# Filling the half-height last chunk of 704 gated values with zeros, up to 128 rows

## The chip, the cores and the metric

The kernel runs on one core of a Trainium2 chip. The metric is the device time of one execution in microseconds (us). The engines are TensorE (PE; its weight loads are listed apart as PEld), VectorE (DVE), ScalarE (ACT), GpSimd (POOL) and SyncE (SP), and SyncE issues most of the DMAs.

## The reference, cut to what matters

Four layers run one after the other on x of shape (4, 512, 256), each a cross-attention and a feed-forward. Two of the feed-forwards have a hidden width of 704. The first layer's is a mixture of 8 experts, two per token:

```python
B, T, D, F = (4, 512, 256, 704)
gate = jnp.einsum('bted,edf->btef', dispatched, gate_proj)
up = jnp.einsum('bted,edf->btef', dispatched, up_proj)
acts = jax.nn.silu(gate) * up
expert_out = jnp.einsum('btef,efd->bted', acts, down_proj)
```

The third layer's rounds its input, its weights and its hidden values to fp4, in blocks of 16 values with one scale each:

```python
gate = fp4_linear(x, w_gate)
y = fp4_linear(x, w_up)
h = jax.nn.silu(gate) * y
return fp4_linear(h, w_down)
```

704 is five and a half times 128. The product with the down weights sums over these 704 values.

## The kernel before

Both places cut the 704 hidden values into FC = 6 chunks: FULL = 5 of 128 rows and a last one of LEFT = 64 rows (FW holds the heights). A chunk stands with its rows on the partitions, and TensorE sums over them.

**The blocks of the first layer** (function `blocks`, names that begin with e0b_). Tokens are sorted by expert into NB = 39 blocks of 128 rows. For each block n TensorE does `gate(n)` (into gp), `turn_rows(n + 1)` (transposes the next block's rows, into xp), `up_product(n)` (into up) and `down(n - 1)` (into yp). An fp32 matmul of the program is two records in the trace, each with its weight load: gate is 24 records with 128 columns, turn_rows 2, up 20, and down 12 with 256 columns, of which the last two are the half-height chunk. The gate product's sixth chunk holds 64 gate columns and, beneath them, the first 64 up columns, so it is full. DVE multiplies (`hidden`: five chunks, then the half chunk) into hT[j], copies the transposed rows (`copy_rows`) and the result (`copy_out`), and every two blocks it does one round of fp4 rounding of the third layer's weights (f2w_). ACT applies silu. SP loads each block's weights into double buffers: wgu[j] is reloaded when `up_product(n)` has ended, for block n + 2, and wd[j] when `down(n)` has. The last layer (e3b_) uses the same function with F = 512, which has no half chunk; for it the new wait and memsets are not made.

**The fp4 feed-forward** (function `lookup_and_feed_forward`, names f_ and f2w_). T = 16 tiles of 128 tokens. The order of TensorE is written out by hand; for tile n it is `gate_up(n)` (tails of 192 columns, then gp, up, then the tails of up, which wait for ACT's silu of the first tails), `turn_rows(n + 1)`, `down(n - 2)`, `turn_hidden(n - 1)`, and in some tiles the parts of a nearest-neighbour lookup. DVE does the multiplication `hidden(n)`, then the rounding of the hidden values of tile n and of the rows of tile n + 2 (some 8 us), then the statistics of tile n - 3 and `add(n - 2)`, which reads yp. POOL ends both roundings (f_hq, f_xq). `turn_hidden` transposes hq by chunks into two groups, hp (four chunks) and hx (chunk 4 and the half chunk, which is a matmul with 64 stationary columns), and ACT's `copy_hidden` takes them to hT: one copy of four chunks, one of chunk 4, one of the half chunk. `down` is 12 records of 256 columns, as in the blocks.

Each stage ends with a barrier, and POOL then clears the stage's semaphores one by one.

Of the kernel before, what the change touches and what calls it, by code (L numbers as in the profile page):

```python
# [21 lines left out]
P = 128  # L22
# [103 lines left out]
def build(nc, ctx, ins, out):  # L126
# [2033 lines left out]
    def blocks(tag, w_gate, w_up, w_down, F, NB, experts_n, owner, token, rounds=None, pair=None):  # L2160
# [14 lines left out]
        with ExitStack() as st:  # L2175
# [22 lines left out]
            if pair is None:  # L2198
# [3 lines left out]
            x_turned, x_copied, gate_made, up_made, sg_done, h_done, y_made, y_copied = (  # L2202
                sem(n) for n in ("xt", "xc", "gate", "up", "sg", "h", "ymade", "yc"))
            DN = 16 if F % P == 0 else 32

            with nc.Block() as block:
                @block.sync
# [90 lines left out]
                @block.tensor  # L2298
                def _(pe):
                    def turn_rows(n, j, count):  # L2300
                        pe.wait_ge(rows_in[j], 16 * before[j] + 16 * count)
                        for k in range(KC):
                            last = nc.tensor.transpose(xp[:, k, :], xb[j][:, k * P:(k + 1) * P], ident)  # L2303
                        last.then_inc(x_turned, 1)

                    def product(at, chunks, dst, j, done):
                        for f in range(chunks):
                            for k in range(KC):
                                last = nc.tensor.matmul(dst[:, f, :], wgu[j][:, k, at + f * P:at + (f + 1) * P], xT[j][:, k, :],  # L2309
                                                        start=(k == 0), stop=(k == KC - 1))  # L2310
                        last.then_inc(done, 1)

                    def gate(n, j, count):
                        pe.wait_ge(x_copied, n + 1)
                        pe.wait_ge(gu_in[j], 32 * count)
                        if positive(n):
                            pe.wait_ge(h_done if LEFT else sg_done, n)
                        product(0, FC, gp, j, gate_made)

                    def up_product(n, j):  # L2320
                        if positive(n):
                            pe.wait_ge(h_done, n)
                        product(F + LEFT, FULL, up, j, up_made)

                    def down(n, j, count):
                        pe.wait_ge(d_in[j], DN * count)
                        pe.wait_ge(y_copied, n + 1)
                        pe.wait_ge(h_done, n + 1)
                        for f in range(FC):
                            last = nc.tensor.matmul(yp[:], hT[j][0:FW[f], f, :], wd[j][0:FW[f], f, :], start=(f == 0),  # L2330
                                                    stop=(f == FC - 1))
                        last.then_inc(y_made, 1)

                    def body(i, last_block=False):
                        for j in (1, 0):
                            n = i * 2 + 2 - j
                            gate(n, j, i + 2 - j)
                            if not (last_block and j == 0):
                                turn_rows(n + 1, 1 - j, i + 2)
                            up_product(n, j)  # L2340
                            down(n - 1, 1 - j, i + 1)

                    stay_busy(gp[:, 0:4, :].rearrange("p f c -> p (f c)"), 30)
                    turn_rows(0, 0, 1)
                    gate(0, 0, 1)
                    turn_rows(1, 1, 1)
                    up_product(0, 0)
                    with pe.Fori(0, NB // 2 - 1) as i:
                        body(i)
                    body(NB // 2 - 1, last_block=True)  # L2350
                    down(NB - 1, 0, NB // 2 + 1)
# [16 lines left out]
                @block.vector  # L2368
                def _(dve):
                    def copy_rows(n, j):  # L2370
                        dve.wait_ge(x_turned, n + 2)
                        nc.vector.tensor_copy(xT[j][:], xp[:]).then_inc(x_copied, 1)  # L2372

                    def hidden(n, j):
                        dve.wait_ge(sg_done, n + 1)
                        dve.wait_ge(up_made, n + 2)
                        for rows, chunks in PIECES:
                            from_up = up[rows, chunks, :] if chunks.start == 0 else gp[P - LEFT:P, chunks, :]
                            last = nc.vector.tensor_tensor(hT[j][rows, chunks, :], from_up, sg[rows, chunks, :], ALU.mult)  # L2379
                        last.then_inc(h_done, 1)  # L2380

                    def copy_out(n, j, count):
                        dve.wait_ge(y_made, n + 2)
                        if positive(count):
                            dve.wait_ge(stored[j], 16 * stored_before[j] + 16 * count)
                        nc.vector.tensor_copy(yb[j][:], yp[:]).then_inc(y_copied, 1)

                    copy_rows(0, 0)
                    copy_rows(1, 1)
                    hidden(0, 0)  # L2390
                    def body(i, last_block=False):
                        for j in (1, 0):
                            n = i * 2 + 2 - j
                            if not (last_block and j == 0):
                                copy_rows(n + 1, 1 - j)
                            hidden(n, j)
                            copy_out(n - 1, 1 - j, i)
                        if rounds is not None and not last_block:
                            rounds.round(dve, i)
                    body(0)  # L2400
                    with dve.Fori(1, NB // 2 - 1) as i:
                        body(i)
                    body(NB // 2 - 1, last_block=True)
                    copy_out(NB - 1, 0, NB // 2)
# [304 lines left out]
    def lookup_and_feed_forward(tag, layer, wt, slot, NB, F, weights):  # L2709
# [4 lines left out]
        with ExitStack() as st:  # L2714
# [10 lines left out]
            moments, root, rstd, shift = ([tmp(f"{n}{k}", s) for k in range(2)] for n, s in (  # L2725
                ("moments", [P, T, 2]), ("root", [P, T]), ("rstd", [P, T]), ("shift", [P, T])))
            xq, xT, sg, h, hq, hT = tmp("xq", [P, D]), tmp("xT", [P, KC, P]), tmp("sg", [P, F]), tmp("h", [P, F]), \
                tmp("hq", [P, F]), tmp("hT", [P, FC, P])
            x_bufs, h_bufs = quantise_buffers(tmp, D), quantise_buffers(tmp, F)
            cb = [ps(f"cb{j}", [P, S]) for j in range(2)]  # L2730
            gp, up, tails, hp0, hx, yp = ps("gp", [P, FM]), ps("up", [P, FM]), ps("tails", [P, 2, FT]), ps("hp", [P, 4, P]), \
# [10 lines left out]
                    "num", "hot", "ht", "hc", "p", "added", "recnt"))  # L2742
            aggregated, rooted, inverted, shifted, xn_ready = ([sem(f"{n}{k}") for k in range(2)] for n in (
                "agg", "root", "inv", "shift", "xn"))
            x_steps, h_steps, both_steps, x_quant, x_turned, x_copied, tail_made, gate_made, up_made, sg_tail, sg_done, h_done, h_quant, \
                h_turned, h_copied, y_made, y_added = (sem(n) for n in (
                    "xs", "hs", "bs", "xq", "xt", "xc", "tail", "gate", "up", "sgt", "sg", "h", "hq", "ft", "fc", "y", "ya"))
# [10 lines left out]
                return (xq[:], xn[:, n, :], D, x_bufs, x_quant, n)  # L2758

            def hidden_job(n):  # L2760
                return (hq[:], h[:], F, h_bufs, h_quant, n)

            with nc.Block() as block:
                @block.gpsimd
# [38 lines left out]
                def _(act):  # L2803
# [43 lines left out]
                    def copy_hidden(n):  # L2847
                        if n:
                            act.wait_ge(y_made, n)
                        for g, chunks in enumerate(groups):  # L2850
                            act.wait_ge(h_turned, n * NG + g + 1)
                            full = [f for f in chunks if FW[f] == P]
                            last = nc.scalar.copy(hT[:, full[0]:full[-1] + 1, :], hp[g][:, 0:len(full), :])
                            for f in chunks:
                                if FW[f] < P:
                                    last = nc.scalar.copy(hT[0:FW[f], f, :], hp[g][0:FW[f], f % 4, :])
                            last.then_inc(h_copied, 1)

                    act.preload_act_table(ACT.Sqrt)
                    act.wait_ge(summed, 1)  # L2860
# [38 lines left out]
                def _(dve):  # L2899
# [65 lines left out]
                    def statistics(n):  # L2965
                        dve.wait_ge(y_added, n + 1)
                        nc.vector.bn_stats(st6[:, n, :], x[:, n, :])

                    for b in range(B):
                        nc.vector.tensor_tensor(sqc[:, b, :], ctx_tok[:, b, :], ctx_tok[:, b, :], ALU.mult).then_inc(c_step, 1)  # L2970
                    dve.wait_ge(c_step, B)
# [52 lines left out]
                def _(pe):  # L3024
# [64 lines left out]
                    def turn_hidden(n):  # L3089
                        pe.wait_ge(h_quant, n + 1)  # L3090
                        for g, chunks in enumerate(groups):
# [2 lines left out]
                            if g:  # L3094
                                pe.wait_ge(x_copied, min(n + 3, T))
                            for f in chunks:
                                last = nc.tensor.transpose(hp[g][0:FW[f], f % 4, :], hq[:, f * P:f * P + FW[f]], ident)
                            last.then_inc(h_turned, 1)

                    def down(n):  # L3100
                        if n:
                            pe.wait_ge(y_added, n)
                        for g, chunks in enumerate(groups):
                            pe.wait_ge(h_copied, n * NG + g + 1)
                            for f in chunks:
                                last = nc.tensor.matmul(yp[:], hT[0:FW[f], f, :], dT[0:FW[f], f, :], start=(f == 0),
                                                        stop=(f == FC - 1))
                        last.then_inc(y_made, 1)

                    pe.wait_ge(c_step, B + 3)  # L3110
                    for b in range(B):
                        for k in range(KC):
# [93 lines left out]
```

## Time and profile before

| | before |
|---|---|
| runs, median (3) | 1820.89 us |
| runs, lowest to highest | 1820.48 to 1825.39 us |
| profiled execution, first to last instruction | 1819.4 us |
| PE busy | 1573.1 us (86%) |
| DVE busy | 983.0 us (54%) |
| ACT / POOL busy | 483.2 / 401.9 us |
| mean granted TensorE clock | 0.944 of 2.4 GHz |

The span of the profiled execution is 1.5 us under the median of the runs; the runs have no profile of their own. An engine's share is a mean over stages that differ, so it says little about any one of them. A record's length is not what it costs a stream of matmuls, because they are pipelined: what counts is the time from one start to the next.

### The profile page before, as it was taken

What the parts mean: (1) busy time and instruction counts of PE and PEld (TensorE: products, weight loads), DVE (VectorE), ACT (ScalarE), POOL (GpSimd) and SP (SyncE); (2) the same over time, 40 slices, a digit from 0 to 9 for tenths busy, and PEclk for the clock granted to TensorE, in tenths of its full rate; (3) what the DMA queues carried; (4) which work ended last, traced back from release to release, by engine and by line L of the source; (5) the groups of instructions that cost most, each with busy time, mean ns of one, the idle gap of its engine ahead of it and who ended that gap; (6) DMA issues with size and microseconds to landing.
All of it is one profiled execution on the core that took longest, in us unless ns stands there. A gap on an engine that the chain in (4) does not pass through costs nothing. (4 is left out here: it accounts for less than half of the span.)

```text
span 1819.4 us, 33679 instructions
## 1 busy us (share of the span) xinstructions
PE 1573.1 (86%) x11798; PEld 1136.1 (62%) x11830; DVE 983.0 (54%) x2513; ACT 483.2 (27%) x1045; POOL 401.9 (22%) x734
## 2 busy tenths in 40 slices
PE   5878999999968988799979899668888887999992
PEld 3654888889857743355544555445655664798992
DVE  4555344444369957766646333479887456222224
ACT  2331101101066631355522111223331431111010
POOL 0102211111042001111102244333111111344440
PEclk9999999999969999899999999878999999999996
DMA  4104888988721007234315132210000001799995
GB/s 141 38 2 145 302 300 292 308 293 301 231 62 36 2 1 195 82 85 110 82 32 168 33 81 77 70 38 18 1 1 1 1 2 47 260 315 318 314 320 187
DMA packets 162223, 240.64 MB, mean 132 GB/s; under 512 B 19808, under 2 KB 109344, under 8 KB 161984
## 3 DMA queue, kind: packets, MB, share of 16 engines
q1 hardware_dynamic: 149440, 208.35, 35.4%
q0 software_dynamic: 10512, 28.72, 5.8%
q10 hardware_dynamic: 2160, 2.10, 0.3%
q8 instruction: 69, 1.13, 0.3%
q14 instruction: 42, 0.34, 0.1%
HBM read 208.96 MB, written 30.15 MB: 131 GB/s over the span
## 5 line engine op out<-in xcount | busy, mean ns | idle before, releaser
L1543 DVE TENSOR_REDUCE l1a_nm<-l1a_sc 128x1 f32<-128x512 f32 (+3 forms) x256 | 107.1, 482 | 53.7 <-PE l1a_sc L1679 53.7
L2309 PEld LDWEIGHTS e0b_gp<-e0b_xT,e0b_wgu 128*128 128x128 f32 x936 | 107.4, 192 | 14.5 <-issue 12.3
L2309 PE MATMUL e0b_gp<-e0b_xT,e0b_wgu 128*128 128x128 f32 x936 | 114.9, 279 | 1.8 <-DVE e0b_hT L2379 1.3
L2330 PE MATMUL e0b_yp<-e0b_wd,e0b_hT 128*128 128x256 f32 x468 | 115.1, 388 | 0.6 <-issue 0.6
L2360 ACT ACTIVATE e0b_sg<-e0b_gp 128x640 f32<-128x640 f32 x78 | 33.5, 481 | 285.3 <-PE e0b_gp L2309 285.3
L2330 PEld LDWEIGHTS e0b_yp<-e0b_wd,e0b_hT 128*128 128x128 f32 x468 | 82.6, 189 | 21.9 <-issue 13.9
L2309 PE MATMUL e0b_up<-e0b_xT,e0b_wgu 128*128 128x128 f32 x780 | 93.5, 275 | 0.0
L2309 PEld LDWEIGHTS e0b_up<-e0b_xT,e0b_wgu 128*128 128x128 f32 x780 | 90.2, 192 | 0.0
L2309 PE MATMUL e3b_gp<-e3b_xT,e3b_wgu 128*128 128x128 f32 x624 | 78.1, 278 | 5.9 <-DMA e3b_wgu<-in_L_ffn_W 4.8
L2309 PEld LDWEIGHTS e3b_gp<-e3b_xT,e3b_wgu 128*128 128x128 f32 x624 | 73.9, 192 | 14.7 <-DMA e3b_wgu<-in_L_ffn_W 7.3
L2464 PE MATMUL e1b_gu<-e_kgu,e1b_xT 128*128 x152 | 75.2, 617 | 4.4 <-DVE e1b_xT L2529 2.8
L2360 ACT ACTIVATE e3b_sg<-e3b_gp 128x512 f32<-128x512 f32 x39 | 23.3, 597 | 206.3 <-PE e3b_gp L2309 206.3
L2309 PE MATMUL e3b_up<-e3b_xT,e3b_wgu 128*128 128x128 f32 x624 | 76.0, 275 | 0.0
L2330 PE MATMUL e3b_yp<-e3b_wd,e3b_hT 128*128 128x256 f32 x312 | 73.9, 380 | 0.6 <-issue 0.6
L2309 PEld LDWEIGHTS e3b_up<-e3b_xT,e3b_wgu 128*128 128x128 f32 x624 | 72.7, 192 | 0.0
L2379 DVE TENSOR_TENSOR e0b_hT<-e0b_up,e0b_sg 128x640 f32<-128x640 f32 x39 | 32.1, 824 | 64.2 <-PE e0b_up L2309 64.2
L1679 PE MATMUL l1a_sc<-causal_h,ident_h 128*128 128x128 bf16 x256 | 47.0, 223 | 20.0 <-PEq L1325 15.6
L1677 PEld LDWEIGHTS l1a_sc<-l_stack_k,l_stack_q 128*128 128x128 bf16 x256 | 25.3, 99 | 61.0 <-issue 27.2
L2330 PEld LDWEIGHTS e3b_yp<-e3b_wd,e3b_hT 128*128 128x128 f32 x312 | 56.3, 190 | 7.0 <-issue 0.9
L2372 DVE COPY e3b_xT<-e3b_xp 128x256 f32<-128x256 f32 x39 | 16.5, 424 | 78.8 <-PE e3b_xp L2303 78.8
L1206 DVE TENSOR_REDUCE a_nm<-a_sc 128x8 f32<-128x512 f32 x64 | 39.7, 682 | 35.8 <-PE a_sc L1056 35.8
L2259 POOL COPY e0b_index<-e_token 128x1 uint32 (+1 forms) x39 | 7.1, 182 | 233.6 <-PE e0b_xp L2303 228.8
(606 smaller groups left out, 3536.3 us busy)
## 6 DMA issues: line engine op xcount, KB each, us to landing
e3b_wgu<-in_L_ffn_W SPq DMA_DIRECT2D x78, 512.0 KB, 5.3
e0b_wgu<-in_L_ffn_gate_proj SPq DMA_DIRECT2D x39, 704.0 KB, 4.4
e0b_wgu<-in_L_ffn_up_proj SPq DMA_DIRECT2D x39, 704.0 KB, 5.8
e0b_wd<-in_L_ffn_down_proj SPq DMA_DIRECT2D x39, 640.0 KB, 5.2
e3b_wd<-in_L_ffn_W SPq DMA_DIRECT2D x39, 512.0 KB, 6.9
x_rows<-xn SPq DMA_DIRECT2D x3, 2048.0 KB, 8.6
l_parts<-l1p_split SPq DMA_DIRECT2D x16, 384.0 KB, 3.1
l_stack_k<-l_parts SPq DMA_DIRECT2D x48, 128.0 KB, 2.8
```

Of the source, the lines that this page charges most:

```text
L1206: nc.vector.tensor_reduce(nm[:, :, r, :], bank[r][:].rearrange("p t (h l) -> p t h l", l=L), AX_X, ALU.max, negate=True).then_inc(max_done, 1)
L1543: nc.vector.tensor_reduce(nm[:, g % 2, q, i:i + 1], sc[q], AX_X, ALU.max, negate=True).then_inc(max_done, 1)
L1677: nc.tensor.matmul(sc[q], of_head(1, n)[:, q * P:(q + 1) * P], of_head(0, n)[:, 0:(q + 1) * P], start=True, stop=False)
L1679: last = nc.tensor.matmul(sc[q][:, q * P:(q + 1) * P], ident_h[:], causal_h[:], start=False, stop=True)
L2259: nc.gpsimd.tensor_copy(index[j][:], token[:, bass.ds(n, 1)]).then_inc(index_ready, 1)
L2309: last = nc.tensor.matmul(dst[:, f, :], wgu[j][:, k, at + f * P:at + (f + 1) * P], xT[j][:, k, :], start=(k == 0), stop=(k == KC - 1))
L2330: last = nc.tensor.matmul(yp[:], hT[j][0:FW[f], f, :], wd[j][0:FW[f], f, :], start=(f == 0), stop=(f == FC - 1))
L2360: last = nc.scalar.activation(sg[rows, chunks, :], gp[rows, chunks, :], ACT.Silu)
L2372: nc.vector.tensor_copy(xT[j][:], xp[:]).then_inc(x_copied, 1)
L2379: last = nc.vector.tensor_tensor(hT[j][rows, chunks, :], from_up, sg[rows, chunks, :], ALU.mult)
L2464: last = nc.tensor.matmul(gu[n % 2][:], xT[n % 2][:, k, :], wgu[:, bass.ds(e, 1), k, :].rearrange("p a f -> p (a f)"), start=(k == 0), sto ...
```

## The change

The last chunk's missing 64 rows are set to zero once, and the instructions then take all 128 partitions. In the blocks, DVE zeroes rows 64 to 127 of the last chunk of hT and wd (both buffers) at the start of the stage, and TensorE waits for these four memsets once, before its loop. The weight DMAs and the multiplication still write rows 0 to 63 alone. In the fp4 feed-forward, hq is widened to 768 columns with the last 64 zeroed, and the last chunk's rows 64 to 127 of dT are zeroed; the last transpose and the last product become full, and ACT copies chunk 4 and the last chunk in one instruction instead of two.

```diff
# blocks
                         for f in range(FC):
-                            last = nc.tensor.matmul(yp[:], hT[j][0:FW[f], f, :], wd[j][0:FW[f], f, :], start=(f == 0),
-                                                    stop=(f == FC - 1))
+                            last = nc.tensor.matmul(yp[:], hT[j][:, f, :], wd[j][:, f, :], start=(f == 0), stop=(f == FC - 1))
...
                     up_product(0, 0)
+                    if LEFT:
+                        pe.wait_ge(padded, 4)
...
+                    for j in range(2 if LEFT else 0):
+                        nc.vector.memset(hT[j][LEFT:P, FULL, :], 0.0).then_inc(padded, 1)
+                        nc.vector.memset(wd[j][LEFT:P, FULL, :], 0.0).then_inc(padded, 1)
                     copy_rows(0, 0)
# lookup_and_feed_forward
-                tmp("hq", [P, F]), tmp("hT", [P, FC, P])
+                tmp("hq", [P, FC * P]), tmp("hT", [P, FC, P])
...
-                            full = [f for f in chunks if FW[f] == P]
-                            last = nc.scalar.copy(hT[:, full[0]:full[-1] + 1, :], hp[g][:, 0:len(full), :])
-                            for f in chunks:
-                                if FW[f] < P:
-                                    last = nc.scalar.copy(hT[0:FW[f], f, :], hp[g][0:FW[f], f % 4, :])
-                            last.then_inc(h_copied, 1)
+                            nc.scalar.copy(hT[:, chunks[0]:chunks[-1] + 1, :], hp[g][:, 0:len(chunks), :]).then_inc(h_copied, 1)
...
+                    nc.vector.memset(hq[:, F:], 0.0).then_inc(padded, 1)
+                    nc.vector.memset(dT[FW[FC - 1]:P, FC - 1, :], 0.0).then_inc(padded, 1)
...
-                                last = nc.tensor.transpose(hp[g][0:FW[f], f % 4, :], hq[:, f * P:f * P + FW[f]], ident)
+                                last = nc.tensor.transpose(hp[g][:, f % 4, :], hq[:, f * P:(f + 1) * P], ident)
...
-                                last = nc.tensor.matmul(yp[:], hT[0:FW[f], f, :], dT[0:FW[f], f, :], start=(f == 0),
-                                                        stop=(f == FC - 1))
+                                last = nc.tensor.matmul(yp[:], hT[:, f, :], dT[:, f, :], start=(f == 0), stop=(f == FC - 1))
...
+                    pe.wait_ge(padded, 2)
                     pe.wait_ge(c_step, B + 3)
```

## Rows read from the trace of the kernel before

**Rows 1.** The page: the span, and PE in 40 slices of it.
```profile
span 1819.4 us, 33679 instructions
...
PE   5878999999968988799979899668888887999992
...
PEclk9999999999969999899999999878999999999996
```

**Rows 2.** Busy time by stretch: the first layer's blocks, the last layer's.
```profile
core 0: us, PE busy (x) PEld busy (x) DVE busy (x) ACT busy (x) POOL busy (x), PEclk, DMA share, GB/s
190.00:470.00 280.00, 280.00 (x2011) 250.44 (x2011) 118.78 (x307) 30.03 (x70) 49.55 (x105) 1.00 0.90 300
1570.00:1770.00 200.00, 195.77 (x1461) 182.68 (x1462) 52.78 (x103) 20.90 (x35) 95.67 (x207) 1.00 0.96 318
```

**Rows 3.** Timeline of one block of the first layer, half-height records on PEld.
```profile
start us, us, engine line op out<-in xcount [idle before <-releaser]
348.53 2.95 PE L2330 MATMUL e0b_yp<-e0b_wd,e0b_hT 128*128 128x256 f32 x12
...
349.36 0.41 SPq L2214 DMA_DIRECT2D e0b_wgu<-in_L_ffn_up_proj  x1
...
350.79 0.29 PEld L2330 LDWEIGHTS e0b_yp<-e0b_wd,e0b_hT 64*128 64x128 f32 x2 [0.33 <-issue]
351.41 2.75 PEld L2309 LDWEIGHTS e0b_gp<-e0b_xT,e0b_wgu 128*128 128x128 f32 x24 [0.33 <-issue]
351.41 2.94 PE L2309 MATMUL e0b_gp<-e0b_xT,e0b_wgu 128*128 128x128 f32 x24
...
354.19 0.38 PE L2303 MATMUL e0b_xp<-consts,e0b_xb 128*128 128x128 f32 x2
...
354.41 2.40 PE L2309 MATMUL e0b_up<-e0b_xT,e0b_wgu 128*128 128x128 f32 x20
...
356.65 0.60 PE L2330 MATMUL e0b_yp<-e0b_wd,e0b_hT 128*128 128x256 f32 x2
...
356.85 0.82 DVE L2379 TENSOR_TENSOR e0b_hT<-e0b_up,e0b_sg 128x640 f32<-128x640 f32 x1 [1.21 <-PE e0b_up L2309]
```

**Rows 4.** Timeline of PE in the last layer's blocks, all chunks full.
```profile
1574.06 1.89 PE L2330 MATMUL e3b_yp<-e3b_wd,e3b_hT 128*128 128x256 f32 x8
1575.78 1.95 PE L2309 MATMUL e3b_gp<-e3b_xT,e3b_wgu 128*128 128x128 f32 x16
1577.57 0.38 PE L2303 MATMUL e3b_xp<-consts,e3b_xb 128*128 128x128 f32 x2
```

**Rows 5.** Groups of the first layer's blocks: the half-height matmuls.
```profile
L2330 PE MATMUL e0b_yp<-e0b_wd,e0b_hT 64*128 64x256 f32 x78 | 27.1, 428 | 0.0
```

**Rows 6.** Timeline, DVE: the first copy of the blocks; a memset elsewhere.
```profile
181.98 0.43 DVE L2372 COPY e0b_xT<-e0b_xp 128x256 f32<-128x256 f32 x1 [9.11 <-PE e0b_xp L2303]
...
968.61 0.17 DVE L2035 MEMSET e1r_lg<- 128x128 f32 x1 [0.82 <-PEq L328]
```

**Rows 7.** DMA issues of the first layer's blocks: KB each, median us to landing.
```profile
e0b_wgu<-in_L_ffn_up_proj SPq DMA_DIRECT2D x36, 704.0 KB, 5.8
```

**Rows 8.** Waits, 1287 to 1401 us: total us, times, longest.
```profile
DVE f_h L2957 <- PE f_tails L3075: 17.5, 10, 4.1
...
PE f_tails L3075 <- ACT f_sg L2843: 8.7, 2, 5.2
```

**Rows 9.** Timeline of the fp4 feed-forward, where PE or DVE waited.
```profile
1287.41 1.65 PE L3075 MATMUL f_tails<-f2w_up,f_xT 128*128 128x192 f32 x4 [5.18 <-ACT f_sg L2843]
...
1356.21 0.44 PE L3070 MATMUL f_hx<-consts,f_xq 128*128 128x128 f32 x2 [1.15 <-POOL f_xq L2621]
...
1365.08 0.36 DVE L2957 TENSOR_TENSOR f_h<-f_tails,f_sg 128x192 f32<-128x192 f32 x1 [1.55 <-PE f_tails L3075]
...
1374.68 0.44 PE L3070 MATMUL f_hx<-consts,f_xq 128*128 128x128 f32 x2 [1.15 <-POOL f_xq L2621]
...
1390.73 4.74 PE L3106 MATMUL f_yp<-f2w_down,f_hT 128*128 128x256 f32 x12 [3.69 <-DVE x L2963]
```

**Rows 10.** Timeline of PE there: transposes, the last with 64 stationary columns.
```profile
1305.26 0.38 PE L3097 MATMUL f_hx<-consts,f_hq 128*128 128x128 f32 x2
1305.48 0.82 PE L3075 MATMUL f_tails<-f2w_gate,f_xT 128*128 128x192 f32 x4
```

**Rows 11.** Timeline of ACT there: the copies of one tile's hidden values.
```profile
1396.14 0.59 ACT L2853 COPY f_hT<-f_hp 128x512 f32<-128x512 f32 x1 [8.34 <-PE f_hp L3097]
1396.62 0.27 ACT L2853 COPY f_hT<-f_hx 128x128 f32<-128x128 f32 x1
1396.78 0.27 ACT L2856 COPY f_hT<-f_hx 64x128 f32<-64x128 f32 x1
```

More of the change, by code:

```diff
@@ L2204, in blocks @@
             DN = 16 if F % P == 0 else 32
+            padded = sem("padded")
             with nc.Block() as block:
@@ L2744, in lookup_and_feed_forward @@
                 "agg", "root", "inv", "shift", "xn"))
+            padded = sem("padded")
             x_steps, h_steps, both_steps, x_quant, x_turned, x_copied, tail_made, gate_made, up_made, sg_tail, sg_done, h_done, h_quant, \
@@ L2760, in hidden_job @@
             def hidden_job(n):
-                return (hq[:], h[:], F, h_bufs, h_quant, n)
+                return (hq[:, 0:F], h[:], F, h_bufs, h_quant, n)
             with nc.Block() as block:
```

## The prediction

> **What bounds the kernel now.** I began with the page's slices [rows 1]: TensorE is at 8 or 9 tenths in nearly every slice from the fourth on, so the two stages that the change touches have to be read by themselves. The stretches come next [rows 2]. From 190 to 470 us, in the first layer's blocks, PE is busy for 280.00 of 280.00 us at a granted clock of 1.00, while DVE does 119 us of work and the DMA engines are 0.90 busy at 300 GB/s. There PE's own stream is the bound, and anything taken out of it shortens the stage one for one, until the weights can't follow. The last layer's blocks, which are the same code without a half chunk, move 318 GB/s at a share of 0.96, and PE is idle for 4.2 of 200 us.
>
> A timeline of one block then shows what a busy PE hides [rows 3]. Before the two half-height weight loads PEld is idle for 0.33 us, and before the first full-height load behind them for 0.33 us again, both put down to "issue": nothing that the profile shows was awaited. Elsewhere in the block the next load lies over the running matmul.
>
> **What a half-height chunk costs.** Starts, not lengths, are compared.
> - Where all chunks are full, 8 records with 256 columns take from 1574.06 to 1575.78, or 0.215 us each, and 16 with 128 columns take 1.79 us, or 0.112 each [rows 4].
> - In the first layer's block, down's 12 records take from 348.53 to 351.41, 2.88 us [rows 3]. At 0.215 they would take 2.58. The loss is 0.30 us.
> - The 24 gate records behind them take from 351.41 to 354.19, 2.78 us, against 24 × 0.112 = 2.69. The loss is 0.09 us, on the first of them. The 20 up records take 2.24 us, exactly 0.112 each, so they lose nothing.
> - Together that is **0.39 us a block**, in a block of 8.12 us (348.53 to 356.65). A block without it would take 7.73 us.
>
> The last layer also ends an accumulation and changes its PSUM bank between down and gate, and loses nothing there. So the loss belongs to the change of height, once on the way in and once on the way out. After the change no block has either.
>
> Here the Trainium skill speaks, in "TensorEngine Tiling (Array Packing)", section Tiling Modes, Key Properties: changing the tiling mode drains TensorE. It lists 64 rows as one mode, with which the row of this block agrees. It lists 128 rows by 64 columns as another, and by that the last transpose of each tile in the fp4 feed-forward would cost such a drain as well. The trace does not bear that out: the pair of transposes with the 64-column one in it takes from 1305.26 to 1305.48, 0.11 us a record as everywhere, and the tails start on time [rows 10].
>
> **The change part by part, the blocks.**
> - 78 half-height records are 39 chunks [rows 5]. 38 of them are followed by more work of the stream, for 38 × 0.39 = 14.8 us. The last one ends the stage and loses only the two steps before its end, some 0.2 us. Sum: **−15.0 us**.
> - A full-height record for a half-height one costs nothing beyond its 0.215 us, which is in the 7.73.
> - The four memsets are under 0.17 us each (a 128x128 one on DVE takes that [rows 6]; these have half the partitions and up to 256 columns, so I take 0.17 to 0.34 each as the upper bound, 1.4 us for all). DVE is idle for 9.11 us before its first copy of the stage [rows 6], so they cost nothing. If that cover were gone they would delay the first block by up to 1.4 us. The new wait of PE is over by then; queued behind it are only the blocks themselves.
> - What is late next: DVE's `hidden` waited 1.21 us for up in the block with a fp4 round before it [rows 3], and the block gets shorter by 0.39, so DVE still waits about 0.8 us. SP issues the second half of wgu at 349.36 and it lands 5.8 us later at the median [rows 7], at 355.2. It is for the gate one block after that of 351.41, at 359.5, so it has 4.3 us to spare, of which 0.39 to 0.8 go.
> - The bytes: 300 GB/s × 8.12 us is 2.44 MB a block. In 7.73 us that is 315 GB/s, at a share of 0.90 × 8.12 / 7.73 = 0.945. Both stay just under the last layer's 318 GB/s and 0.96. I take no cost, and keep the other end for the rivals.
>
> **The fp4 feed-forward.** The same 0.39 us stands at each of its 16 downs, but here DVE and PE hold each other up, so only those on the path count. DVE is filled until PE's tails of 1287.41, which themselves waited 5.18 us for ACT, behind DVE [rows 9]. Until there (the first four downs) I count nothing. From there on, DVE waits for PE's tails ten times, 17.5 us in all [rows 8]: PE is on the path of almost every tile. Of the twelve downs left,
> - three lie before the next wait for ACT and one behind it in a tile whose end PE sets: 4 × 0.39 = 1.56;
> - one lies before that second wait of PE's tails for ACT [rows 8], whose chain comes from DVE, and one before the 3.69 us wait for DVE at 1390.73 [rows 9]: nothing;
> - in the last regular tiles, PE waits 1.15 us for POOL's f_xq in every second tile, 18.47 us apart, and DVE waits 1.55 us for PE in between [rows 9]. The loop DVE, POOL, PE goes over two tiles and holds one down, so of these four downs two count: 0.78;
> - the down of 1390.73 counts in full, 0.39, and the last to its end, 0.20.
>
> Sum: **−2.9 us**. The bounds are the last two alone (−0.6) and all sixteen (15 × 0.39 + 0.2, −6.0). The transpose becomes wider at no cost [rows 10]. The ACT copies shrink from three to two. The third starts 0.16 us behind the second and takes 0.27 [rows 11]; 384 more columns take 0.32 us, so 128 more take about 0.1, and less than 0.1 us is won. Only in the very last tile does PE wait for them, and there for the first group alone. The two memsets come at the stage's start, where DVE goes on to wait for gathered rows; bound 0 to 0.5 us, taken as 0.
>
> **Clock.** The mean granted clock is 0.944. Everything behind the first layer moves 15 us forward, and a different stretch may fall on the clock's low level (1.2 of 2.4 GHz). No row prices that. At 0.944, about 0.112 × 1819 = 204 us lie at the low level, and if one or two per cent of that changes, it is 2 to 4 us of either sign. I take 0 and put ±3 into the range.
>
> **Sum.** 1819.4 − 15.0 − 2.9 = 1801.5 us of span. The median of the runs lies 1.5 above the span, so 1803.0 us.
>
> **The rivals.**
> - *The weights come late.* For: 315 GB/s would be at 99% of what the last layer reaches, and there PE is idle for 2.1% of the time [rows 2]. Against: the loads have 3.5 us or more to spare, and the last layer also moves a scattered write from POOL. The same 2.1% of 38 × 7.73 = 294 us would take 6.2 us back: 1809. Chance 0.12.
> - *Narrow stationary operands drain too*, by the page's rule. As a mechanism of this kernel: each tile's last transpose would lose 0.39 like a down, and as much again is won in the feed-forward: 1800. The row against it is [rows 10]. Chance 0.03.
> - *The change doesn't do what it says.* If the 0.33 us idle times come from something else in the last chunk, such as its end of an accumulation, they stay: 1820 to 1821. The last layer's rows speak against it [rows 4]. Chance 0.03.
> - *Slower.* The DMA engines could lose throughput when blocks crowd. The point that decides is 300 GB/s, the present rate: below it a block takes longer than 8.12 us. At 290 GB/s it is 2.44 MB / 290 = 8.41 us, 38 × 0.29 = 11 us more, less the 2.9: 1829. Against: the last layer holds 318 with more, smaller transfers. Chance 0.02.
> - *The forecast*: 1803, chance 0.80.
>
> **How the numbers follow.** The forecast's own spread is −0.6 to −6.0 in the feed-forward and ±3 for the clock, about 1799 to 1807. The late weights lift the upper end to 1809. The rivals at 1820 and 1829 lie outside, as does a part of each tail. A measurement of this kernel tells 0.3%, 5.5 us, from no change. The forecast, the late weights and the transposes are faster by more than that: 0.95. No change 0.03, slower 0.02.
>
> **What would show it.** Right: no 64*128 loads and no 0.33 us idle time in front of the gate's first load; blocks 7.73 us apart; 190 to 455 us still without a gap on PE; DMA near 315 GB/s at 0.95; DVE waiting about 0.8 us for up; in the feed-forward 0.2 us less per tile on average behind 1287 us. Wrong: gaps on PE that end with a DMA of e0b_wgu; a full-height last chunk that still starts 0.31 us after the one before it; low clock in slices that now have none.

## The result, and the profile after

| | before | changed |
|---|---|---|
| median of the runs | 1820.89 us (4) | 1805.52 us (4) |
| lowest to highest | 1820.48 to 1825.39 | 1803.55 to 1809.65 |
| profiled span | 1819.4 us | 1803.9 us |
| first layer's blocks, stage | 330.4 us | 315.4 us |
| fp4 feed-forward, stage | 243.9 us | 239.4 us |

The changed kernel takes 0.9911 of the time before, with a 95% interval of 0.9889 to 0.9933: 15.4 us less. A stage's length here and below is the time from POOL's first clearing of semaphores at the end of the stage before (line 104) to the same at its own end.

The page of the changed kernel, its span and the granted clock in 40 slices, to be held against [rows 1]:

```profile
span 1803.9 us, 33705 instructions
...
PEclk9998999999969998999989999879999998999996
```

Four slices that were at 9 are now at 8 (the 4th, the 16th, the 21st and the 34th), and two that were at 8 are at 9. Low clock in new slices was one of the prediction's signs of being wrong. Summed over the execution the time at the low clock is nearly the same, 204.8 us against 203.0 us before.

Busy time by stretch of the changed kernel, the first layer's blocks and then the last layer's, against [rows 2]:

```profile
190.00:450.00 260.00, 260.00 (x1958) 249.66 (x1957) 114.61 (x294) 29.18 (x68) 51.27 (x102) 1.00 0.95 315
1555.00:1755.00 200.00, 193.69 (x1446) 181.37 (x1445) 53.09 (x104) 20.31 (x35) 94.15 (x203) 1.00 0.96 316
```

PE is still without a gap in the blocks, but it starts 7.53 records a us where it started 7.18 before, and the DMA engines now move 315 GB/s at a share of 0.95. Both figures are those of the prediction. One block in the timeline of the changed kernel, against [rows 3]:

```profile
340.71 2.46 PEld L2332 LDWEIGHTS e0b_yp<-e0b_wd,e0b_hT 128*128 128x128 f32 x12
340.82 2.75 PE L2332 MATMUL e0b_yp<-e0b_wd,e0b_hT 128*128 128x256 f32 x12
...
343.20 2.86 PEld L2310 LDWEIGHTS e0b_gp<-e0b_xT,e0b_wgu 128*128 128x128 f32 x24
343.41 2.84 PE L2310 MATMUL e0b_gp<-e0b_xT,e0b_wgu 128*128 128x128 f32 x24
...
346.09 0.38 PE L2304 MATMUL e0b_xp<-consts,e0b_xb 128*128 128x128 f32 x2
...
348.54 1.68 PE L2332 MATMUL e0b_yp<-e0b_wd,e0b_hT 128*128 128x256 f32 x7
348.74 0.82 DVE L2382 TENSOR_TENSOR e0b_hT<-e0b_up,e0b_sg 128x640 f32<-128x640 f32 x1 [1.01 <-PE e0b_up L2310]
```

The reader is to see that gate's first weight load (343.20) now starts 0.21 us ahead of gate's first matmul (343.41), under down's last one. Before the change the two started together, after 0.33 us of idle time. Down takes 2.59 us from start to start (2.88 before), gate 2.68 (2.78 before), and the whole block 7.72 us (8.12 before). In these two executions DVE waits 1.01 us for up in the block with a fp4 round, and 1.21 us before. The other blocks with such a round agree within 0.02 us, but for the first and the last of them.

### The profile page after: what moved, and what is told of

Read it like the earlier page. It is cut to its first block and busy times, and to the rows that moved or that the text cites. A ratio compares the mean times of both kernels' runs of the same rounds, so it can differ in the third digit from the quotient of the medians.

```text
span 1803.9 us, 33705 instructions
## 1 busy us (share of the span) xinstructions
PE 1557.8 (86%) x11830; PEld 1146.5 (64%) x11830; DVE 984.0 (55%) x2519; ACT 482.8 (27%) x1029; POOL 405.4 (22%) x734
## 5 line engine op out<-in xcount | busy, mean ns | idle before, releaser
L2310 PE MATMUL e0b_gp<-e0b_xT,e0b_wgu 128*128 128x128 f32 x936 | 111.0, 275 | 1.8 <-DVE e0b_hT L2382 1.3
L2332 PE MATMUL e0b_yp<-e0b_wd,e0b_hT 128*128 128x256 f32 x468 | 107.5, 379 | 0.6 <-issue 0.6
L1677 PE MATMUL l1a_sc<-l_stack_k,l_stack_q 128*128 128x512 bf16 (+3 forms) x256 | 59.1, 309 | 18.2 <-PEq L1325 16.4
L2541 DVE TENSOR_TENSOR e1b_h<-e1b_gu,e1b_sg 128x256 f32<-128x256 f32 x38 | 16.1, 423 | 78.6 <-ACT e1b_sg L2524 78.6
```

Of the source, the lines that this page charges most:

```text
L1677: nc.tensor.matmul(sc[q], of_head(1, n)[:, q * P:(q + 1) * P], of_head(0, n)[:, 0:(q + 1) * P], start=True, stop=False)
L2332: last = nc.tensor.matmul(yp[:], hT[j][:, f, :], wd[j][:, f, :], start=(f == 0), stop=(f == FC - 1))
L2541: nc.vector.tensor_tensor(h[n % 2][:], gu[n % 2][:, F:2 * F], sg[n % 2][:], ALU.mult).then_inc(h_done, 1)
```

## The experiments

**1 and 2. The two parts apart.** One kernel has the padding in `blocks` alone, the other in `lookup_and_feed_forward` alone; the edit is the half of the diff above that belongs to the function.

> The padding in the first layer's blocks alone, the fp4 feed-forward as before. Theory (each change of height costs TensorE, 0.39 us a block, and the blocks are bound by its stream): 15 us less than before, blocks 7.73 us apart, the feed-forward's stage as long as before, 243.9 us. Rival (most of the gain came from elsewhere in the program): less than 12 us.

> The padding in the fp4 feed-forward alone. Theory of the prediction: 2.9 us less in that stage (241.0 us). Rival (what the traces of before and after differ by is all due to the padding): 4.5 us less in that stage (239.4 us). Second rival (the stage's length depends on where the low clock falls in it, which moved with the 15 us): the stage is between these and its low-clock slices lie where they did before.

**3 and 4. Both kernels again.** No edit.

> The kernel before, profiled a second time, to see by how much each stage differs between two executions of one program. If the differences seen in stages that the change does not touch (-1.6 us in the second attention, +1.9 in the third layer's, +1.6 in the last layer's blocks) are chance, differences of this size show up here as well; if they come from the change, stages repeat within 0.3 us.

> The changed kernel, profiled and timed again. As for the kernel before: if stages that the change does not touch differ from the first trace of this kernel by 1 to 2 us, their differences are chance. Time: 0.991 of before.

Against the kernel before on the same chip (median 1823.95 us of 17 runs), the blocks alone take 0.9901 of its time (interval 0.9863 to 0.9939, median 1807.06 us), the feed-forward alone 0.9967 (0.9945 to 0.9990, median 1820.28 us), and the changed kernel 0.9881 (0.9843 to 0.9919, median 1803.41 us). The 0.991 that was expected of the changed kernel lies in its interval. Stage lengths in us, worked out from the traces, with the part of each that lies at the low clock (1.2 GHz) in brackets:

```
                      before       before again  changed      changed again blocks only  ffn only
first attention       114.7 (10.2) 116.2 (13.7)  114.7 (10.2) 114.8 (10.2)  114.7 (10.2) 114.2 (10.2)
first layer's blocks  330.4 (2.9)  331.0 (5.2)   315.4 (2.9)  315.4 (3.0)   316.0 (5.3)  330.9 (5.2)
second attention      149.1 (34.1) 146.6 (27.3)  147.4 (34.1) 147.6 (30.7)  148.9 (33.7) 148.6 (30.7)
third attention       213.1 (11.6) 212.4 (12.3)  215.0 (14.7) 212.3 (12.1)  212.7 (12.2) 212.3 (12.0)
fp4 feed-forward      243.9 (64.9) 243.8 (64.9)  239.4 (61.4) 240.2 (58.0)  243.8 (64.9) 240.3 (54.6)
last layer's blocks   245.1 (9.6)  245.1 (9.6)   246.7 (11.2) 243.0 (10.9)  245.3 (9.7)  246.0 (10.4)
```

("third attention" is the latent attention of the second layer's feed-forward; the expectation of the repeated kernel calls it the third layer's.) Four things follow. With the padding in the blocks alone they are 7.72 us apart (7.73 expected) and the feed-forward's stage is as long as before. The blocks' stage repeats within 0.6 us for the same code and falls by 14.9 to 15.0 us between executions with the same low-clock time (330.4 to 315.4, 331.0 to 316.0). The feed-forward's falls by 3.5 to 4.5 us; with the padding there alone it has 240.3 us, between the 241.0 of the theory and the 239.4 of the rival, but its time at the low clock is not what it was before (54.6 and 64.9 us), so the length alone decides neither. And stages with the same code differ by 1 to 3 us between executions, mostly where their time at the low clock differs: the kernel before gave 149.1 and 146.6 us for the second attention, and the changed one 215.0 and 212.3 for the third. So the differences of 1 to 2 us that the first pair of traces shows elsewhere are chance, as the expectation for the repeated kernels had it. The last layer's blocks had the same 245.1 to 245.3 in the three executions with the old feed-forward and 243.0 to 246.7 in those with the new one. That is no trend either: the next two experiments, with the old feed-forward, gave 243.9 and 247.1.

**5. The half chunk in another place.** The kernel before, in `down` of the blocks:

```diff
-                        for f in range(FC):
-                            last = nc.tensor.matmul(yp[:], hT[j][0:FW[f], f, :], wd[j][0:FW[f], f, :], start=(f == 0),
-                                                    stop=(f == FC - 1))
+                        order = [0, 1, FC - 1] + list(range(2, FC - 1)) if LEFT else list(range(FC))
+                        for f in order:
+                            last = nc.tensor.matmul(yp[:], hT[j][0:FW[f], f, :], wd[j][0:FW[f], f, :], start=(f == order[0]),
+                                                    stop=(f == order[-1]))
```

> The kernel before, with the half-height chunk third instead of last in down's sum, in the first layer's blocks. Theory (the loss is at each change of height, wherever it stands): the same 0.39 us a block, blocks 8.11 us apart, stage 330.4 us; the 0.33 us idle times of the weight loads now both stand inside down, and gate's 24 records take 2.69 us instead of 2.78. Rival (the loss belongs to the end of the sum, or to the step from down to gate): the first idle time stays at the last chunk or the loss vanishes, blocks 7.7 to 7.9 us apart.

The stage took 330.7 us, and the one run 1823.44 us, against 1823.43 us for one run of the kernel before on the same chip. Its timeline:

```profile
343.88 3.15 PE L2331 MATMUL e0b_yp<-e0b_wd,e0b_hT 128*128 128x256 f32 x12
344.83 0.29 PEld L2331 LDWEIGHTS e0b_yp<-e0b_wd,e0b_hT 64*128 64x128 f32 x2 [0.33 <-issue]
345.46 1.16 PEld L2331 LDWEIGHTS e0b_yp<-e0b_wd,e0b_hT 128*128 128x128 f32 x6 [0.33 <-issue]
...
346.86 2.84 PE L2309 MATMUL e0b_gp<-e0b_xT,e0b_wgu 128*128 128x128 f32 x24
...
349.54 0.38 PE L2303 MATMUL e0b_xp<-consts,e0b_xb 128*128 128x128 f32 x2
```

Both idle times have moved into the middle of down, which now takes 2.98 us, 0.39 more than with full chunks, and gate takes 2.68, as in the changed kernel. The loss follows the height. It belongs neither to the end of the sum nor to the step from down to gate.

**6. One more half chunk.** The kernel before, with the third chunk's rows 64 to 127 left out of the sum:

```diff
                         for f in range(FC):
-                            last = nc.tensor.matmul(yp[:], hT[j][0:FW[f], f, :], wd[j][0:FW[f], f, :], start=(f == 0),
-                                                    stop=(f == FC - 1))
+                            high = P // 2 if LEFT and f == 2 else FW[f]
+                            last = nc.tensor.matmul(yp[:], hT[j][0:high, f, :], wd[j][0:high, f, :], start=(f == 0),
+                                                    stop=(f == FC - 1))
```

> The kernel before, in whose blocks the third chunk of down is taken at half height as well: rows 64 to 127 of that chunk are left out of the sum. No other work changes. Theory (each change of height costs): two more changes a block, 0.39 us more, blocks 8.51 us apart, stage 345.6 us, 15 us slower than before, although less is computed. Rival (a half-height record is simply slower than a full one, by half of 0.39 us, or the loss comes once a block): blocks 8.11 to 8.3 us apart.

The stage took 345.6 us, 15.2 more than before, and the program 1837.23 us in its one run, 13.8 more than the run of the kernel before. Its timeline shows every change of height:

```profile
347.05 3.34 PE L2331 MATMUL e0b_yp<-e0b_wd,e0b_hT 128*128 128x256 f32 x12
...
348.01 0.29 PEld L2331 LDWEIGHTS e0b_yp<-e0b_wd,e0b_hT 64*128 64x128 f32 x2 [0.33 <-issue]
348.64 0.73 PEld L2331 LDWEIGHTS e0b_yp<-e0b_wd,e0b_hT 128*128 128x128 f32 x4 [0.33 <-issue]
349.70 0.29 PEld L2331 LDWEIGHTS e0b_yp<-e0b_wd,e0b_hT 64*128 64x128 f32 x2 [0.33 <-issue]
350.32 1.86 PEld L2309 LDWEIGHTS e0b_gp<-e0b_xT,e0b_wgu 128*128 128x128 f32 x16 [0.33 <-issue]
```

Down now takes 3.27 us from its start to gate's (347.05 to 350.32), where it took 2.88. Half a chunk less to multiply made each block 0.39 us longer. The size of the loss is set by the number of times the height changes, twice for each half chunk between full ones.

**7 and 8. How near the weights are to a bound.** The changed kernel with less work for TensorE and the same bytes. In the first two of the up product's five chunks (in the second kernel, in the first four) only the first half of D is summed:

```diff
-                            for k in range(KC):
+                            depth = 1 if LEFT and dst is up and f < 2 else KC
+                            for k in range(depth):
...
-                                                        start=(k == 0), stop=(k == KC - 1))
+                                                        start=(k == 0), stop=(k == depth - 1))
```

> The changed kernel, in whose blocks two of the ten matmuls of the up product are left out (the first two chunks are summed over half of D). 0.45 us less of TensorE's work a block, so that blocks would be 7.28 us apart if TensorE still bounds them, which asks for 2.44 MB / 7.28 = 334 GB/s. Theory (the weights had room for the change, but not much more): the blocks end between 7.28 and 7.65 us apart, PE gets idle times that a DMA of e0b_wgu ends, and the rate stays at 318 to 325 GB/s. Rival (the weights are far from a bound): 7.28 us, no idle time of PE.

> As the one before with four of the ten matmuls of the up product left out. TensorE's work would be 6.83 us a block, which asks for 356 GB/s. Theory: the weights bound the blocks, 7.4 to 7.7 us apart, nearly as with two left out, at 318 to 325 GB/s. Rival: 6.83 us.

Busy time from 190 to 430 us, of the kernel with two left out and then of the one with four:

```profile
190.00:430.00 240.00, 240.00 (x1784) 229.77 (x1783) 113.41 (x292) 28.32 (x66) 50.04 (x99) 1.00 1.01 333
...
190.00:430.00 240.00, 238.37 (x1742) 226.06 (x1743) 119.40 (x309) 30.05 (x70) 52.06 (x105) 1.00 1.03 350
```

and what PE waited for in that stretch of the second:

```profile
PE e0b_gp L2311 <- DMA e0b_wgu<-in_L_ffn_up_proj: 1.6, 3, 1.0
PE e0b_gp L2311 <- DVE e0b_hT L2383: 1.3, 1, 1.3
```

Both of my expectations fell. With two matmuls left out PE has no gap at 333 GB/s. With four it waits for weights three times, 1.6 us in 240, at 350 GB/s, and its blocks are 6.83 us apart at the median. (The wait for DVE of 1.3 us stands at the stage's start in the other kernels too.) The stages took 298.5 and 285.3 us, against 315.4 for the changed kernel. The weights had room for far more than this change: the first waits for them appear at 350 GB/s. The share of 0.95 to 0.96 that I had read as nearly full is no ceiling: the same column reads 1.01 and 1.03 here.

**9 and 10. The feed-forward's parts apart.** The kernel before with only the transposes made full, and with only the products made full. The ACT copies stay as they were in both, and both have the two memsets and the wait for them. In the first:

```diff
-                tmp("hq", [P, F]), tmp("hT", [P, FC, P])
+                tmp("hq", [P, FC * P]), tmp("hT", [P, FC, P])
...
-                                last = nc.tensor.transpose(hp[g][0:FW[f], f % 4, :], hq[:, f * P:f * P + FW[f]], ident)
+                                last = nc.tensor.transpose(hp[g][:, f % 4, :], hq[:, f * P:(f + 1) * P], ident)
```

> Of the change the last transpose of the fp4 feed-forward alone is made full (hq widened), with the copies, the products and the blocks as before. Theory (64 stationary columns do not cost what 64 rows do): the feed-forward's stage stays at 243.8 us, with records of the transposes 0.11 us apart. Rival, by the rule of the tiling page that every change of tiling mode drains: 3 us less, 240.9 us.

> Of the change the products of the fp4 feed-forward alone are made full, with the transposes and copies as before (the unused rows of hT zeroed once) and the blocks as before. Theory: the whole gain of the feed-forward, 3.5 us, stage 240.3 us. Rival (the transposes or the shorter copies of ScalarE carry some of it): 241 us or more.

The single runs took 1819.42 us with the transposes and 1824.89 with the products, against 1819.38 for the kernel before on the same chip; the second is 5.5 us longer although its stage got shorter, since other stages, whose code is the same, came out long (214.8 us for the third attention, 247.8 for the last layer's blocks). The feed-forward's stage took 239.6 us with the transposes and 239.5 with the products, so by its length alone each would have had the whole gain. That can't be, and the low clock is why the length misleads here: 51.2 us of it with the transposes and 61.4 with the products, against 64.9 before. What remains is to compare a stretch at full clock. DVE's `hidden` of the tiles numbered 7 and 9 has two downs on PE between them and waits for PE at the end. These are its starts in the kernel before, with the transposes alone, and with the products alone:

```profile
1299.28 0.36 DVE L2957 TENSOR_TENSOR f_h<-f_tails,f_sg 128x192 f32<-128x192 f32 x1 [1.74 <-PE f_tails L3075]
...
1322.94 0.36 DVE L2957 TENSOR_TENSOR f_h<-f_tails,f_sg 128x192 f32<-128x192 f32 x1 [1.29 <-PE f_tails L3075]
```

```profile
1297.58 0.36 DVE L2958 TENSOR_TENSOR f_h<-f_tails,f_sg 128x192 f32<-128x192 f32 x1 [1.29 <-PE f_tails L3078]
...
1321.24 0.36 DVE L2958 TENSOR_TENSOR f_h<-f_tails,f_sg 128x192 f32<-128x192 f32 x1 [1.28 <-PE f_tails L3078]
```

```profile
1299.98 0.36 DVE L2958 TENSOR_TENSOR f_h<-f_tails,f_sg 128x192 f32<-128x192 f32 x1 [0.88 <-PE f_tails L3078]
...
1322.93 0.36 DVE L2958 TENSOR_TENSOR f_h<-f_tails,f_sg 128x192 f32<-128x192 f32 x1 [0.97 <-PE f_tails L3078]
```

They are 23.66, 23.66 and 22.95 us apart: the transposes give nothing, and two full downs give 0.71 (0.76 in the changed kernel).

The same can be done for the whole stage. Its length is cut in three at DVE's `hidden` of the first and of the last tile, and the tiles numbered 12 to 14, all at full clock, are given beside it (us from the traces, low clock in brackets):

```
                 to the first   first to last   behind the last  tiles 12 to 14
before           55.29 (34.1)   171.11 (27.3)   17.49 (3.4)      18.47
before again     55.29 (34.1)   171.02 (27.3)   17.49 (3.4)      18.48
changed          52.96 (27.3)   168.67 (27.3)   17.77 (6.8)      18.13
changed again    55.76 (30.7)   167.47 (23.9)   16.95 (3.4)      18.13
transposes only  52.75 (27.3)   168.32 (17.1)   18.54 (6.8)      18.48
products only    52.70 (27.3)   169.18 (27.3)   17.59 (6.8)      18.13
```

Up to the first `hidden` no down has run, so the 2.3 us that the changed kernel is shorter there in its first execution are not the padding's; its second execution is 0.5 us longer there than the kernel before. Between the first and the last `hidden`, with the same 27.3 us at the low clock, the change wins 2.44 us, and behind the last one, with the same 3.4 us, 0.54: together 3.0 us. (An equal time at the low clock need not fall on the same instructions, so this is good to some tenths of a us; the products alone win 1.9 in the first of the two.) The transposes alone have the old distance over two tiles (18.48), the products alone the new one (18.13). What made the stage short with the transposes alone is the low clock: the first two pieces hold 17 us less of it than before and are 5.3 us shorter.

The Trainium skill says, in "TensorEngine Tiling (Array Packing)", Key Properties, that changing the tiling mode drains TensorE. The traces agree for 64 rows (0.39 us for the way in and out) and not for 64 columns, where full transposes won nothing; whether a load with 64 stationary columns is run in another mode at all, no row shows.

## Why the prediction was right

It said 1803.0 us, and the runs gave 1805.52; the span was to be 1801.5 and was 1803.9. Both terms of the sum are borne out by the traces. That the total came so near is in part luck: the changed kernel's runs lie between 1800.06 and 1809.65 us, and it was 15.4 us faster than the kernel before in the first comparison and 20.5 in the second (medians), with 17.9 foretold.

- *The blocks, −15.0 us.* The stage fell by 14.9. Blocks 8.12 to 7.72 us apart (7.73 foretold), down 0.29 us and gate 0.10 us shorter (0.30 and 0.09), 315 GB/s at 0.95. Experiments 5 and 6 show the cause: each change between 64 and 128 rows on TensorE, wherever it stands.
- *The memsets.* The four took 0.17 or 0.27 us each, at 173 to 174 us, so the "under 0.17" of the prediction was too low and its 0.17 to 0.34 right, and DVE then still waited for PE before its first copy, for 7.62 us. The kernel's time holds nothing of them.
- *DVE's wait for up.* It was to be about 0.8 us and is 1.01. The prediction took the whole 0.39 off it. But DVE's work before that wait begins with the copy of down's result, and this comes 0.20 us earlier too (2.99 us behind down's first record before, 2.79 after). Only the step behind down's end is left to shorten the wait.
- *The weights come late* (rival, 0.12). No. The arithmetic was right (315 GB/s), the ceiling was wrong. I had taken the last layer's 318 GB/s as near what the DMA engines can do, and experiments 7 and 8 moved 333 and 350. Why the last layer's PE waits for its weights at 316 to 318 GB/s was not tried.
- *The feed-forward, −2.9 us.* The stage was 243.7 to 243.9 us in the five executions without any of the change in it. In the five with all of it (experiments 7 and 8 have it too) it was 239.4 to 241.2, 240.2 on average, so it fell by 3.6 us on average. At equal time at the low clock it is 3.0 us, as the table of experiments 9 and 10 has it, so the term was right for the padding; the rest is the clock's, which the sum had at nothing in this stage. The walk behind the term held where it can be read: 0.38 us a down at full clock, nothing for the downs before the wait for ACT (the first `hidden` to the seventh take 76.7 to 76.8 us in all twelve executions), and 0.34 us over two of the last regular tiles, where it had 0.39.
- *The narrow transposes* (rival, 0.03): refuted by experiment 9, *the change doesn't do what it says* (0.03) by experiments 5 and 6 and by the 14.9 us of the blocks, *slower by crowding* (0.02) by 7 and 8.
- *The clock, 0 ± 3 us.* Elsewhere the first pair of traces lost 4 us of what the two stages won (14.9 + 4.5 = 19.4 against 15.5 of span): 1.9 and 1.4 in and behind the third attention, 1.6 in the last layer's blocks, with 1.6 won in the second attention. The repeated kernels show such differences for the same code.

What stays open is why the low clock falls where it does. The feed-forward's first piece had 34.1 us of it in four of the five executions with the old stage and 27.3 or 30.7 in the seven in which some of the change stood in it. One program gave both 27.3 and 30.7, so part of this is chance; whether the edit shifts it as well is not shown.

## What to carry to other kernels

Look in a timeline for weight loads that don't overlap the matmul before them although nothing is awaited; where the number of rows changes there, TensorE loses some 0.2 us each time, and zero rows up to the common height cost nothing. Do it where TensorE's stream sets the pace: the same edit gave its full 0.39 us a time in the blocks, and about half of that over all in the stage where DVE and PE wait for each other (3.0 us over 16 downs). And before a gain of a few us is read off a stage's length, compare the time it spent at the low clock, and where: the feed-forward had 61.4 us of it both in experiment 5, with 243.9 us, and with the products alone, with 239.5. A distance between two instructions in a stretch at full clock is the surer measure.

## What the runs showed of the hardware that was not expected

- The DMA engines moved 350 GB/s over 240 us in experiment 8, where the last layer's blocks of the kernel before had 318. The DMA share read 1.03 then, so a share near 1 does not say that they are full.
- At the low clock a change of height stands out more: with the transposes alone, at the down of 1386.65 us, PEld is idle for 0.65 us before the half-height loads and again before the next full one, where it is idle for 0.33 us at full clock.
- Where the low clock falls differs between executions of one program: the second attention had 34.1 us of it and then 27.3, and the feed-forward between 51.2 and 64.9 over twelve executions. The stage of 243.8 us with 64.9 and that of 239.6 with 51.2 had the same half-height products. Part of the spread of the runs goes with it: of 17 runs of the kernel before on one chip, the fifteen between 1820.84 and 1826.97 us have mean granted clocks of 0.946 to 0.941, the longer ones the lower by tendency (correlation −0.63), and one of 1843.73 us has 0.900. The seventeenth took 7311.21 us at 1.000, which is not the clock's doing and stays unexplained.
